# Expert feed-forward of a MoE layer: x transposed by VectorE from tiles loaded by quarters, half-row products of the down projection made for two pairs at once

## What is computed

```
x: (8, 512, 512) f32, so T = 4096 tokens of H = 512

x = x + attention(layernorm(x))          # 32 heads of 16, 8 of keys and values, a compressive memory
n = layernorm(x)
scores  = sigmoid(n @ router_w.T)        # 16 experts
chosen  = top 4 of scores + e_bias; c = scores of these, divided by their sum, zero elsewhere
routed  = sum over e of c[:, e] * ((silu(g_e) * u_e) @ down_e.T),  g_e, u_e = n @ gate_up_e.T    # I = 192
shared  = (silu(n @ Sg.T) * (n @ Su.T)) @ Sd.T                     # one more expert for all tokens, I = 192
out     = x + routed + shared
```

## Time and profile before

| | |
|---|---|
| median of three runs | 1956.91 us (1956.83 to 1957.64) |
| the profiled execution | 1947.51 us |
| its span | 1945.6 us |
| TensorE busy | 1872.0 us, 96% |
| VectorE, ScalarE, GpSimd busy | 1031.1, 978.7, 921.2 us |
| mean granted clock of TensorE | 0.985 |
| feed-forward, bodies 0 to 87 | from 1097.9 us to the end |
| one routed body | 9.34 us |

### The profile page before, as it was taken

The page is one execution under the profiler, slowest core; times in us unless marked ns, Lnnn a source line. Parts: engine busy times, 40 slices in busy tenths (PEclk is TensorE's granted clock), DMA queues, the critical chain, the costliest instruction groups (busy, mean ns, idle before and its releaser), DMA issues. The chain is left out here.

```text
span 1945.6 us, 34872 instructions
## 1 busy us (share of the span) xinstructions
PE 1872.0 (96%) x9240; PEld 965.8 (50%) x9241; DVE 1031.1 (53%) x1995; ACT 978.7 (50%) x1901; POOL 921.2 (47%) x1127
## 2 busy tenths in 40 slices
PE   6899999999999999999999899999999999999996
PEld 5444445444544454445333455555555555555553
DVE  5667777878787878787888252222221222222213
ACT  3366776677667766776766532223332233322330
POOL 3533566666666766675633650333333333333342
PEclk9799999999999999999999999999999999999998
DMA  6422334434443444333532897877777777777779
GB/s 193 108 70 64 83 94 132 128 107 116 132 134 103 116 131 135 104 103 120 150 120 82 290 342 237 183 142 141 141 144 142 142 141 141 143 143 141 142 164 262
DMA packets 159128, 277.71 MB, mean 143 GB/s; under 512 B 28704, under 2 KB 64800, under 8 KB 156256
## 3 DMA queue, kind: packets, MB, share of 16 engines
q1 hardware_dynamic: 108688, 147.61, 26.7%
q0 software_dynamic: 40880, 106.96, 26.6%
q10 hardware_dynamic: 9440, 21.68, 3.2%
HBM read 145.65 MB, written 135.74 MB: 145 GB/s over the span
## 5 line engine op out<-in xcount | busy, mean ns | idle before, releaser
L993 DVE TENSOR_REDUCE mx<-ps_max 128x2 f32<-128x1024 f32 x512 | 618.1, 1219 | 174.7 <-PE ps_max L1203 160.6
L732 ACT ACTIVATE prob<-ps_exp 128x512 f32<-128x512 f32 x992 | 566.9, 598 | 149.2 <-PE ps_exp L1217 131.6
L1948 PE MATMUL ps_gu<-wts_sb,xT 128*128 x1152 | 402.7, 493 | 1.2 <-issue 1.0
L1217 PE MATMUL ps_exp<-qs,ks 98*128 98x512 bf16 x992 | 380.0, 383 | 18.9 <-ACT prob L732 16.7
L1647 POOL DMA_INDIRECT out<-yt,idx x72 | 111.7, 1551 | 467.6 <-ACT yt L1716 453.2
L1203 PE MATMUL ps_max<-ks,qs 96*128 96x512 bf16 x1024 | 310.2, 385 | 7.5 <-DVE mx L993 4.0
L1828 DVE COPY hT<-ps_h 128x384 f32<-128x384 f32 x88 | 49.1, 557 | 463.2 <-PE ps_h L1957 463.2
L1948 PEld LDWEIGHTS ps_gu<-wts_sb,xT 128*128 128x128 f32 x1152 | 207.3, 190 | 170.9 <-issue 56.4
L1245 PE MATMUL ps_pv<-prob,vs 128*32 128x512 f32 x2048 | 251.8, 605 | 0.2 <-ACT prob L740 0.2
L1706 ACT ACTIVATE gs<-ps_gu 128x192 f32<-128x192 f32 x176 | 58.2, 330 | 376.4 <-PE ps_gu L1948 376.4
L1217 PEld LDWEIGHTS ps_exp<-qs,ks 98*128 98x128 bf16 x992 | 96.8, 98 | 195.7 <-ACT prob L732 88.5
(11 more groups left out here) (197 smaller groups left out, 2177.2 us busy)
## 6 DMA issues: line engine op xcount, KB each, us to landing
xt<-rows_by_expert SPq DMA_DIRECT2D x144, 264.5 KB, 2.7
dnr_sb<-in_dnr SPq DMA_DIRECT2D x144, 128.0 KB, 2.6
qk_parts<-parts POOLq DMA_DIRECT2D x112, 120.0 KB, 3.6
qs<-qk_parts SPq DMA_DIRECT2D x64, 192.0 KB, 3.1
wts_sb<-in_wts ACTq DMA_DIRECT2D x12, 1024.0 KB, 8.3
x_sb<-in_x SPq DMA_DIRECT2D x16, 512.0 KB, 4.5
qs<-qk_parts SPq DMA_DIRECT2D x64, 128.0 KB, 3.1
x_plus_memory<-am SPq DMA_DIRECT2D x16, 512.0 KB, 5.2
```

Source lines behind the costliest of these rows:

```text
L732: act.activation(prob[:, s, q], ps_exp[:, q % 2], ACT.Exp, scale=SCALE).then_inc(s_exp, 1)
L993: dve.tensor_reduce(mx[:, k % 2, 4 * s + 2 * p:4 * s + 2 * p + 2], ps_max[:, p], AX_X, ALU.max).then_inc(s_maxd, 1)
L1217: pe.matmul(ps_exp[:, q % 2], ks[0:ROWS + MROWS, kk, s * P:(s + 1) * P], qs[0:ROWS + MROWS, kk, q], start=True, stop=True).then_inc(s_sc, 1)
L1948: mm = pe.matmul(ps_gu[:, i, 0:2 * I], xT[:, i, d], w, start=(d == 0), stop=(d == DC - 1))
```

## The change

Four things are changed.

1. **x transposed by VectorE.** `transpose_x` on TensorE and `x_out` on ScalarE go. VectorE transposes each tile with one instruction (`x_out`, 128 partitions by 512, in blocks of 32 by 32) straight from `xt` to `xT`, behind `hidden` of the same tile number. Since it transposes within 32 partitions, the tile is loaded by quarters: four DMAs of 32 partitions, each with 4 runs of 128 numbers (512 bytes) for a partition. The rows of the gate and up weights are permuted on the host to match. The 17 numbers behind x in a row of `XS` go to a tile of their own, `xw`, by one more DMA of 68 bytes a row.
2. **Who loads.** From pair H0 + 2 = 12 on, ScalarE's queue issues the five DMAs of tile 1, between the two silus, and SyncE those of tile 0. Before that SyncE issues all. The loads wait for VectorE's transposes (`s_xT`) where they waited for TensorE's.
3. **Half rows for two pairs.** `ps_y` has four banks. The full products of a pair are made in each body as before; the half-row products are made in every second body, for two pairs one behind the other, through pair 81. `hT` is double. The y copies of ScalarE, the row additions of GpSimd behind them and the loads of `dnr_sb` come in the same rhythm, two pairs in every second body. The late pairs stay as they were.
4. **Order.** On VectorE `weights` and `tokens` move to the head of the body, ahead of `hT_out`. On TensorE the expert numbers of pair h-1 are read between gate-up and down, not at the head of the body.

```diff
-    lent("room_in_x_sb", [P, 6 * D - 4 * RW])
+    xt = lent("xt", [P, 4, D])
+    hT = lent("hT", [P, 2, 3, P])
...
-    ps_x = own.enter_context(nc.psum_tensor("ps_x", [P, 2, DC, P], F32))
-    ps_y = own.enter_context(nc.psum_tensor("ps_y", [P, 2, D], F32))
+    ps_y = own.enter_context(nc.psum_tensor("ps_y", [P, 4, D], F32))
...
+            self.together = not known or h < H1
...
+    def load_quadrants(eng, pair, i, rows):
+        for a in range(QD):
+            part = slice(a * QD_ROWS, (a + 1) * QD_ROWS)
+            eng.dma_start(xt[part, pair.slot(i)].rearrange("t (b d) -> t b d", b=QD),
+                          rows[:, a * P:(a + 1) * P].rearrange("(b t) d -> t b d", t=QD_ROWS)).then_inc(s_x[pair.slot(i)], 16)
+
+    def load_tile(eng, pair, i):
+        if pair.kind == SHARED:
+            load_quadrants(eng, pair, i, XN2[bass.ds(pair.t[i], 1)].rearrange("o p d -> (o p) d"))
+        else:
+            row = eng.value_load(tab[0:1, 0, bass.ds(pair.j[i], 1)], min_val=0, max_val=ZERO_ROW)
+            eng.dma_start(xw[:, pair.slot(i)], XS[bass.ds(row, P), D:RW]).then_inc(s_xw[pair.slot(i)], 16)
+            load_quadrants(eng, pair, i, XS[bass.ds(row, P), 0:D])
+
+    def on_act(later):
+        return not isinstance(later.h, int) or later.h >= H0 + 2
+
+    def whole(pair):
+        if not pair.exists or pair.together and pair.par == 0:
+            return []
+        return [Pair(pair.h - 1, pair.q, 0), pair] if pair.together else [pair]
...
# sync
         def load_x(pair):
-            for i in range(2):
...
+            for i in range(1 if on_act(pair) else 2):
+                load_tile(sp, pair, i)
...
-                wait(s_xp, 2 * pair.h + 2)
+                wait(s_xT, 2 * pair.h + 2)
...
-            if following.exists and following.kind == ROUTED:
-                after(wait, s_yp, following.h - 1)
-                load_rest(following)
+            if pair.par == 1 and pair.kind == ROUTED:
+                wait(s_yp, pair.h - 1)
+                for ready in (before, pair):
+                    load_rest(ready)
# scalar
             silu(pair, 0)
             last_units(chain, pair, "a")
+            if later.exists and on_act(later):
+                act.wait_ge(s_xT, 2 * pair.h + 2)
+                act.sem_inc(s_acg, 1)
+                if pair.kind == ROUTED:
+                    act.wait_ge(s_tok, pair.routed + 1)
+                    act.sem_inc(s_acg, 1)
+                load_tile(act, later, 1)
             silu(pair, 1)
-            if following.exists:
-                x_out(following)
             last_units(chain, pair, "b")
-            if before.exists and not before.both:
-                y_out(before)
+            for ready in whole(before):
+                if not ready.both:
+                    y_out(ready)
...
# vector
+        def x_out(pair, i):
+            dve.wait_ge(s_x[pair.slot(i)], 16 * QD * (pair.q + 1))
+            after(dve.wait_ge, s_gu, 2 * pair.h + i - 1)
+            dve.transpose(xT[:, i].rearrange("p c (b t) -> p c b t", b=QD),
+                          xt[:, pair.slot(i)].rearrange("p (b c d) -> p c b d", b=QD, c=DC)).then_inc(s_xT, 1)
...
                 last.then_inc(s_h, 1)
+                if following.exists:
+                    x_out(following, i)
...
         def body(before, pair, following, later):
+            if pair.kind == ROUTED:
+                weights(pair)
+                tokens(pair)
             if before.exists:
                 hT_out(before)
...
# tensor
-        def transpose_x(pair):
...
         def down(pair, es):
             pe.wait_ge(s_hT, pair.h + 1)
-            after(pe.wait_ge, s_y, 2 * pair.h)
+            after(pe.wait_ge, s_y, 2 * (pair.h - 1))
+            for i in range(2):
+                w = sdn_sb[:] if pair.kind == SHARED else of_expert(es[i], slice(W - D, W))
+                pe.matmul(y_of(pair, i), hT[:, pair.par, i], w, start=True, stop=False)
+            for ready in whole(pair):
+                down_rest(ready)
+
+        def down_rest(pair):
             if pair.kind == ROUTED:
                 pe.wait_ge(s_dn[pair.par], 32 * (pair.q - H0 // 2) + 32)
             for i in range(2):
...
-                mm = pe.matmul(ps_y[:, i], hT[half, 2], w, start=False, stop=True)
+                mm = pe.matmul(y_of(pair, i), hT[half, pair.par, 2], w, start=False, stop=True)
             mm.then_inc(s_yp, 1)
...
-            if following.exists:
-                transpose_x(following)
             if before.exists:
-                down(before, e_before)
+                down(before, experts(before))
```

More of the change, by code:

```diff
@@ L1382, in feed_forward @@
     sgu_sb, sdn_sb, sdnr_sb = (keep[k] for k in ("sgu", "sdn", "sdnr"))
+    xw = keep["xw"]
     token, idx, wpick, wsel, tab, small, smi, padf, padi = (keep[k] for k in (
@@ L1421, in feed_forward @@
     s_x = [sem(f"f_x_loaded{r}") for r in range(4)]
+    s_xw = [sem(f"f_x_weights_loaded{r}") for r in range(4)]
     s_dn = [sem(f"f_down_rest_loaded{p}") for p in range(2)]
-    s_xp = sem("f_xT_in_psum")
     s_xT = sem("f_xT")
@@ L1462, in __init__, with y_of @@
             self.routed = h - H0
+            self.together = not known or h < H1
         def slot(self, i):
             return 2 * self.par + i
+    def y_of(pair, i):
+        return ps_y[:, pair.slot(i)]
     L0, L1 = H0 + 6, H1 - 2
@@ L1694, in scalar @@
     def scalar(act):
[L1695 to L1700, removed]
         def silu(pair, i):
@@ L1745, in body @@
             last_units(chain, pair, "a")
+            if later.exists and on_act(later):
[5 more added lines that the diff above has]
+                load_tile(act, later, 1)
             silu(pair, 1)
-            if following.exists:
-                x_out(following)
             last_units(chain, pair, "b")
-            if before.exists and not before.both:
-                y_out(before)
-            if before.exists and before.kind == SHARED and not before.late:
-                store(before)
+            for ready in whole(before):
+                if not ready.both:
+                    y_out(ready)
+            for ready in whole(before):
+                if ready.kind == SHARED and not ready.late:
+                    store(ready)
             if before.both:
@@ L1838, in weights, with hidden @@
             dve.wait_ge(s_wp, 2 * pair.routed + 2)
-        def hidden(pair):
+        def hidden(pair, following):
             for i in range(2):
@@ L1877, in y_sum @@
             for i in range(2):
-                dve.tensor_tensor(late_y(pair, i), ps_y[:, i], sums[:, n, i], ALU.add).then_inc(s_y, 1)
+                dve.tensor_tensor(late_y(pair, i), y_of(pair, i), sums[:, n, i], ALU.add).then_inc(s_y, 1)
         def body(before, pair, following, later):
+            if pair.kind == ROUTED:
+                weights(pair)
+                tokens(pair)
             if before.exists:
@@ L1883, in body @@
             last_units(chain, pair, "a")
-            if pair.kind == ROUTED:
-                weights(pair)
-            hidden(pair)
+            hidden(pair, following)
             last_units(chain, pair, "b")
-            if pair.kind == ROUTED:
-                tokens(pair)
             if before.exists and before.kind == ROUTED:
@@ L1919, in tensor @@
     def tensor(pe):
-        def transpose_x(pair):
-            for i in range(2):
-                slot = pair.slot(i)
-                pe.wait_ge(s_x[slot], 16 * pair.q + 16)
-                after(pe.wait_ge, s_xT, 2 * pair.h + i - 1)
-                for d in range(DC):
-                    mm = pe.transpose(ps_x[:, i, d], xt[:, slot, d * P:(d + 1) * P], identf[:])
-                mm.then_inc(s_xp, 1)
         def experts(pair):
@@ L1965, in down @@
             for i in range(2):
-                w = sdn_sb[:] if pair.kind == SHARED else of_expert(es[i], slice(W - D, W))
-                pe.matmul(ps_y[:, i], hT[:, i], w, start=True, stop=False)
-            for i in range(2):
                 half = slice(i * IR, (i + 1) * IR)
                 w = sdnr_sb[half] if pair.kind == SHARED else dnr_sb[half, pair.par]
-                mm = pe.matmul(ps_y[:, i], hT[half, 2], w, start=False, stop=True)
+                mm = pe.matmul(y_of(pair, i), hT[half, pair.par, 2], w, start=False, stop=True)
             mm.then_inc(s_yp, 1)
@@ L1976, in body @@
                 pe.wait_ge(s_tab, 1)
-            e_before, e = experts(before), experts(pair)
+            e = experts(pair)
             gate_up(pair, 0, e[0])
```

37 lines of the change are left out of this document (16 added, 21 removed).

## The result

The changed kernel takes 1881.18 us (median, 1876.07 to 1888.55) against 1957.28 (1956.83 to 1960.67) for the kernel before: ratio 0.961, 95% interval 0.9575 to 0.9646. The forecast was 1883.5 and faster. The profiled execution took 1878.89 us, its span 1877.1: 68.6 less than the profiled one of before, where 73.4 were forecast.

What follows compares the result with a forecast made beforehand. TensorE was taken to bound the routed bodies from end to end. Bodies 10 to 82 save 74.5 us, those before 3, the tail loses 4.1: together 73.4, from 1956.9 to 1883.5 us, range 1866 to 1912.

Steps and rivals of the forecast that it cites:

- TensorE's body: Routed bodies: x transposes save 0.87 us, pairing half rows 0.15 (bounds 0 and 0.2), from 9.34 to 8.32 us.
- VectorE: Routed bodies: each transpose of x takes 0.7 us (bounds 0.4 and 1.22), ends before it is wanted, costs nothing.
- one of the signs by which the prediction was to be wrong: Routed bodies: TensorE waits for VectorE's transposes with a load behind them, which would mean transfers bind.
- ScalarE: Routed bodies: five issues, waits and register load take 3.0 us between the silus; silu 1 0.4 us late, cost nothing.
- SyncE: Routed bodies: five DMAs a body and four half-row ones in every second take some 3.5 us of 8.3; cost nothing.
- The rival in which issues bind: Routed bodies: at 1.36 us an issue ScalarE's body is 9.36 us, no change, about 1957 us; chance 0.04.
- The transfers: Routed bodies: small packets at 25 ns, 115 engine-us a body, 7.2 us of 16 engines, below 8.32, barely.
- the 1 in 100 for its result: Routed bodies: by the skill page's 0.95 us for 64 KB, body 12.5 us, kernel about 2190; chance 1 in 100.
- Additions: Routed bodies, GpSimd: row additions land in some 5 us; two pairs need some 12 of 16.6 us; nothing in steady state.
- Ahead of the routed pairs: Bodies 0 to 9: TensorE gains 8.7 us, SyncE's issues and transfers take some 5; 3 kept (bounds -4 and +8.7).
- The tail: Behind the last routed pair: two pairs' additions at the end land 4.1 us later, a loss of 4.1 us.
- The step to the median: Whole kernel: the 73.4 us saving, summed against the profiled execution, is taken from the median 1956.9, giving 1883.5 us.

Runs made afterwards that it cites:

- x1: Changed kernel with half-row products, and their loads, made in every body for its own pair again: 1891.53 us, ratio 0.968 to the kernel before.
- x0: The changed kernel once more, no edit: 1879.37 us, ratio 0.9619 to the kernel before.
- x4: Changed kernel with each quarter loaded by two DMAs of 16 rows, runs still 512 bytes: 1966.58 us, ratio 1.0057 to the kernel before.
- x6: Changed kernel with SyncE issuing all loads, ScalarE none (second change undone): 2009.48 us, ratio 1.0276 to the kernel before.
- x2: Changed kernel with each quarter loaded as 32 whole rows of 2048 bytes, a quarter of the packets: 1881.63 us, ratio 0.9625 to the kernel before.
- x5: Changed kernel with one DMA a tile of x, 128 rows of 2048 bytes: 1877.18 us, ratio 0.9593 to the kernel before.
- x7: Changed kernel with half-row products ordered tile 0, 0, 1, 1 instead of 0, 1, 0, 1: 1883.33 us, ratio 0.9631 to the kernel before.
- x8: Changed kernel with the last two routed pairs' half-row products each in its own body: 1878.94 us, ratio 0.9655 to the kernel before.
- x9: Changed kernel with zero rows written as 4 + 4 + 4 in three bodies instead of 6 + 6: 1882.34 us, ratio 0.9679 to the kernel before.
- third group: The last four follow-up runs, on one chip, where the kernel before had a median of 1945.9 us.
- x10: Changed kernel with ScalarE also issuing tile 1 for shared pairs 2 to 9: 1878.88 us, ratio 0.9656 to the kernel before.
- x11: Changed kernel with last two routed pairs apart, zero rows 4 + 4 + 4, and ScalarE issuing shared tile 1: 1875.85 us, ratio 0.9641 to the kernel before.

## Why the prediction was right

**TensorE's body: right, with the saving at its upper bound.** The forecast was 9.34 - 0.87 - 0.15 = 8.32 us. The 0.87 went in full. Of the half rows the bounds were 0 and 0.2 and the choice 0.15; x1 shows 0.17 (8.463 against 8.29) to 0.20 (by the chains). The Trainium skill's rule (page "TensorEngine Tiling (Array Packing)", section "Key Properties") that a change of the tiling mode drains TensorE stood for this bound, and the trace agrees: the excess, 0.20 on the way in and 0.20 on the way out, is there once per block however long the block is. Measured are 1.07 us a body from body 16 to 80. Over the bodies 10 to 81 it is 77.2 in the first profile and 71.7 in x0, where 73 x 1.02 = 74.5 were forecast; these are 72 bodies, and the sum's 73 count one too many, 1.0 us.

**VectorE: right.** The transpose's group after:

```profile
L1863 DVE STREAM_TRANSPOSE xT<-xt 128x512 f32<-128x512 f32 x176 | 123.5, 702 | 24.6 <-DMA xt<-xn_rows 20.1
```

0.70 us, the elementwise 128x512 of the earlier trace rows (685 ns) almost to the point; the estimate of 1.24 us from the Trainium skill's page "VectorE: DVE Perf Modes", section "The three transpose paths", was too long. Of its 24.6 us of waits 20.1 are for x of shared tiles; in the two routed bodies shown it is not on the chain. In body 10 of x0 TensorE did wait for it, with a load behind it. That is one of the signs by which the prediction was to be wrong; it cost 3.3 us once and not something in each body.

**ScalarE: cost nothing, though its term was too small.** A timeline of the body without half rows, after:

```profile
1408.61 1.55 POOL L1676 DMA_INDIRECT out<-yt,idx  x1 [6.16 <-ACT yt L1738]
...
1410.59 0.33 ACT L1728 ACTIVATE gs<-ps_gu 128x192 f32<-128x192 f32 x1 [1.55 <-PE ps_gu L1977]
...
1411.72 4.41 SPq L1563 DMA_DIRECT2D dnr_sb<-in_dnr  x4
...
1412.25 0.37 ACTq L1503 DMA_DIRECT2D xw<-rows_by_expert  x1
1412.78 1.85 ACTq L1494 DMA_DIRECT2D xt<-rows_by_expert  x4
...
1414.38 1.55 POOL L1676 DMA_INDIRECT out<-yt,idx  x1 [2.37 <-DMA out<-yt,idx]
...
1414.74 0.33 ACT L1728 ACTIVATE gs<-ps_gu 128x192 f32<-128x192 f32 x1 [3.82 <-issue]
```

Between the silus lie 3.8 us (1410.92 to 1414.74), not 3.0, and silu 1 starts 1.36 us behind the end of gate-up of tile 1 (1413.38), not 0.4. Its product, 0.9 us later, is wanted by the transposes of hidden at 1417.68, so some 2 us of room were left. In x4, with 6.2 us in that place, ScalarE is late as well, though SyncE is what binds.

**SyncE: the term that failed, unpunished.** "Some 3.5 us of 8.3" is 0.5 us for each of seven issues, with nothing for the register loads and what else lies between them. By the distances in x6 a tile takes 3.4 us and the half rows of two pairs 6.2: 2 x 3.4 + 6.2 = 13.0 in two bodies of 16.6, 6.5 a body. With all four tiles it is 4 x 3.4 + 6.2 = 19.8 (measured 20.2). SyncE's own waits after, from 1400 to 1600 us (total us, times, longest):

```profile
SPq L1549 <- DVE xT L1863: 19.4, 12, 2.1
SPq L1549 <- DVE token L1895: 14.3, 18, 1.8
```

It waits for 33.7 us of 200, so the queue has less room than the sum says: 17% of the time. The rival in which issues bind was named for the wrong engine and at the wrong price (1.36 us an issue): it needs only 0.5 us an issue with its gap and the register loads, on a queue that carries all. What kept it away is the second change, which the prediction took as free and not as the condition of the gain: without it the kernel is at 2009, slower than before.

**The transfers: right in the sum.** Queues from 1400 to 1600 us after, columns as in the earlier trace rows:

```profile
DMA packets 45586, 32.18 MB, mean 161 GB/s; under 512 B 11558, under 2 KB 36262, under 8 KB 45586
...
q0 software_dynamic: 6965, 12.69, 46.5%
q1 hardware_dynamic: 21191, 12.92, 26.5%
q10 hardware_dynamic: 17430, 6.57, 15.2%
```

q10 is ScalarE's queue: 15.2% of 3200 engine-us for 17430 packets is 28 ns each (25 forecast). A body of 8.29 us has 132.6 engine-us; all three queues take 88.2% of them, 117 (115 forecast), and q1 with q10 41.7% (39 forecast). The Trainium skill's page "DMA: Bandwidth & Descriptors", section "Bandwidth", has 0.95 us of the engines for 64 KB, measured on loads of 128 partitions issued by GpSimd; this queue took 486 engine-us for 96 quarters and 24 small loads, 0.32 us of all 16 a quarter. The measurement decides; the 1 in 100 for its result was enough. x2 (share 0.84 from 1400 to 1500 us) and x5 (0.79) have the same bodies, so the 0.88 was no bound either.

**Additions: nearly right.** They were to land in some 5 us; the second to `out` waits from 1408.61 for the first and goes at 1414.38, 5.8 us. The four fill some 14.6 of the 16.6 us (the last is issued at 1417.21, 8.6 behind the first, and lands some 6 later), not 12. How short a body they would allow no run tests; SyncE's queue (83% of the time without a wait) and the transfers (0.88) stand as near behind TensorE.

**Ahead of the routed pairs: right on the late load, silent on the clock, and not told from scatter.** From body 0 to body 10 the changed kernel took 94.4 and 95.3 us in two profiles where before took 97.3 in one: 2.9 and 2.0 gained, 3 forecast. But x6, x7 and x8, with the same loads up to there, took 95.3, 94.4 and 101.4, so that some 3 came out is in part luck. It was told that SyncE's issues and the transfers would take the rest. The chain there after:

```profile
1162.50 0.47 SPq L1494
1163.02 0.63 SPq L1494
1163.70 0.93 SPq L1494
1164.68 14.44 DMA xt<-xn_rows
1179.14 0.72 DVE xT L1863
1179.90 4.85 PE ps_gu L1977 x8
```

A load of x takes 14.44 us to land, 15.37 in the earlier trace rows. TensorE is idle for 4.9 us, from 1175.0, as the "some 5 us later" has it, and gate-up behind it takes 4.85 instead of 2.6 or 2.8, since the granted clock had fallen to the lower level (1.2 GHz) in the wait:

```profile
1177.10:1183.90 6.80, 4.00 (x6) 2.18 (x7) 3.41 (x5) 0.00 (x0) 0.52 (x1) 0.50 1.05 344
```

This clock is a term that the prediction put at nothing: some 2 us here, and the clock is at 0.50 from 1098.6 to 1108.8 too, where in the kernel before it is 1.00 in both stretches. Neither longer packets (x2) nor fewer DMAs (x5) nor a spread of the zero rows (x9) moved the start of body 10 by more than the scatter. The traffic of weights and zero rows at 0.95 of the engines remains as a cause; it wasn't tried, and that it is the cause isn't shown. The test that the prediction set, body 10 not later than 1195, did fail in the first profile (1198.5) and barely in x0 (1195.6): it was bound to an absolute time, and body 0, in code that the change doesn't touch, had started 6.2 us later.

**The tail: right, 1.3 us too small.** 5.4 and 4.9 us in two profiles (4.1 forecast). After:

```profile
1802.97 1.08 PE ps_y L2004 x4
...
1807.43 5.84 DMA second_sum_rows<-yt,idx
...
1814.05 4.61 DMA second_sum_rows<-yt,idx
```

Two additions to one sum in a row, 5.84 and 4.61, between the last half rows and the joins, as foreseen; x1 and x8, with one pair at a time at the end, have 77.2 and 77.1, so 4 us of it are the pairing. The prediction took the joins before, at 1888.29, as released by the landed additions; the line in the earlier trace rows names TensorE's half rows, and the last addition had landed 0.7 us earlier, at 1887.5.

**The step to the median: two errors that met.** The sum was 4.8 us above the difference of the profiled executions (68.6): the bodies gave 2.7 more than forecast, the tail took 1.3 more, and the stretch up to body 10 gave 6.3 less, nearly all of it the late body 0. The saving of the medians was 76.1. In the third group the kernel before had 1945.9 us, as its profiled execution (1947.5), and in the others 1954.7 to 1957.3; x0 in the first and x8 in the third (1879.4 and 1878.9, one edit apart) don't show this step. So the saving is 67 us or 75 to 76, depending on the group, each of them one chip, and 1883.5 came within 2.3 us partly by luck. What makes the groups differ stays open.

## What to carry to other kernels

Count the cost of an issuing queue from one start to the next in its timeline, not from its recorded durations: here 0.34 us are 0.5, and a set of five with its register load 3.4. A change that multiplies small DMAs can fill the queue that issues them: here its gain on TensorE could be had only with the issues split over two queues. Products at half height cost one entry and one exit per block (0.20 us each here), so put blocks together, and move the loads and additions that go with them, at the end of the loop too.

## Not expected of the hardware

- x0, the same kernel, reached body 0 at 1100.3 us, the first profile at 1104.1, the third group at 1094.4 to 1097.9, the kernel before at 1097.9. In the first profile the granted clock was lower just ahead of body 0, where before it was full:

```profile
1060.00:1080.00 20.00, 16.75 (x94) 6.88 (x91) 10.79 (x23) 11.17 (x21) 13.19 (x13) 0.83 0.62 219
```

  x0 and x7 had 0.83 in the same stretch; in the third group x8, x9, x10 and x11 had 0.99, 1.00, 1.00 and 0.91, and before had 1.00. So it goes with the group more than with the change; what makes it stays open.
- Loads with a quarter of the packets took almost as much of the engines: 15.2% of them at 512 bytes and 13.2% at 2048 on q10 (x2), for the same bytes. With packets of 2048 bytes and one DMA a tile instead of four (x5) it was 10.8%.
- Two half-height products in the same half follow each other as closely as in different halves (x7, 1.92 us for eight either way).
